# Sliding descriptor picks and a four-product tail in a two-layer convolution kernel

## The reference

```python
def spatial_descriptor(x, k):                      # k = 5
    xp = jnp.pad(x, ((0, 0), (0, 0), (2, 2), (2, 2)))
    corrs = [jnp.sum(x * dynamic_slice(xp, (0, 0, di, dj), (b, c, h, w)), axis=1)
             for di in range(k) for dj in range(k)]
    return jnp.stack(corrs, axis=1)                # 25 values at each pixel
def _L0_conv_ref(x, W, bias):
    gs = spatial_descriptor(x, 5)
    gs = gs / jnp.sqrt(jnp.sum(gs * gs, axis=1, keepdims=True) + 1e-6)
    feat = jnp.concatenate([x, gs], axis=1)        # 512 + 25 channels
    return relu(einsum('bchw,oc->bohw', feat, W) + bias)
x = x + _L0_conv_ref(_gn(x), L0_conv_W, L0_conv_bias)
x = x + _L1_conv_ref(_gn(x), ...)                  # pooling windows chosen per plane, mixed
```

## Time and profile before

| what | value |
|---|---|
| median of three runs | 4177.26 us (4173.68 to 4180.9) |
| the profiled execution, its own time | 4180.08 us |
| its span in the profile | 4177.9 us |
| busy, share of the span: TensorE | 83% |
| VectorE | 81% |
| GpSimd | 50% |
| ScalarE | 47% |
| TensorE weight loads (beside its products) | 47% |
| mean rate of all transfers | 187 GB/s |

### The profile page before, as it was taken

The page is one execution under the profiler, slowest core; times in us unless marked ns, Lnnn a source line. Parts: engine busy times, 40 slices in busy tenths (PEclk is TensorE's granted clock), DMA queues, the critical chain, the costliest instruction groups (busy, mean ns, idle before and its releaser), DMA issues. The chain is left out here.

```text
span 4177.9 us, 72982 instructions
## 1 busy us (share of the span) xinstructions
PE 3474.2 (83%) x22600; PEld 1981.8 (47%) x22601; DVE 3378.0 (81%) x3619; ACT 1981.8 (47%) x3227; POOL 2087.4 (50%) x1576
## 2 busy tenths in 40 slices
PE   4999999999999999999999996567678666666554
PEld 3666666666665666666666664223233222222221
DVE  5777777777777777777777766899989999999995
ACT  3545445445445545545445440664556544444342
POOL 3555555556555555555555541554444444454343
PEclk9999999999999999999999996878889888877777
DMA  5445445445454454455455233664478666565552
GB/s 195 154 156 185 164 157 187 158 164 181 161 175 168 165 176 166 162 177 178 147 177 187 98 128 74 258 244 186 184 293 339 269 254 244 232 247 197 222 199 81
DMA packets 252355, 782.10 MB, mean 187 GB/s; under 512 B 98150, under 2 KB 98150, under 8 KB 229990
## 3 DMA queue, kind: packets, MB, share of 16 engines
q1 hardware_dynamic: 219600, 417.85, 29.0%
q0 software_dynamic: 32288, 358.95, 21.9%
HBM read 428.22 MB, written 409.08 MB: 200 GB/s over the span
## 5 line engine op out<-in xcount | busy, mean ns | idle before, releaser
L1039 DVE TENSOR_TENSOR arena<-arena 128x2048 f32<-128x2048 f32 (+9 forms) x635 | 1454.8, 2319 | 66.4 <-issue 23.1
L439 POOL TENSOR_TENSOR arena<-arena 128x512 f16<-128x512 f32 x512 | 651.2, 1277 | 861.5 <-ACT arena L582 860.3
L1390 PE MATMUL psum<-arena 128*128 128x512 f32 x896 | 534.9, 682 | 461.5 <-issue 336.6
L448 POOL TENSOR_TENSOR arena<-arena 128x512 f32 (+1 forms) x512 | 639.7, 1271 | 293.6 <-ACT arena L594 288.2
L1219 PE MATMUL psum<-arena 128*128 128x512 f16 x2048 | 776.3, 379 | 1.0 <-ACT arena L594 1.0
L1221 PE MATMUL psum<-arena 128*128 128x512 f16 x2048 | 776.2, 379 | 0.0
L1220 PE MATMUL psum<-arena 128*128 128x512 f16 x2048 | 776.2, 379 | 0.0
L1196 PE MATMUL psum<-arena 128*128 128x256 f16 (+1 forms) x6344 | 712.7, 270 | 34.5 <-DVE arena L789 21.2
L580 ACT ACTIVATE arena<-arena,gbias,grstd 128x512 f32 (+1 forms) x512 | 413.7, 808 | 632.0 <-PE psum L1221 515.6
L1392 PE MATMUL psum<-arena 128*128 128x512 f32 x1072 | 604.5, 661 | 71.1 <-ACT psum L665 54.4
L679 ACT ACTIVATE arena<-psum 128x512 f32<-128x512 f32 x536 | 315.9, 598 | 716.4 <-PE psum L1392 704.4
(11 more groups left out here) (150 smaller groups left out, 3246.6 us busy)
## 6 DMA issues: line engine op xcount, KB each, us to landing
arena<-in_x SPq DMA_DIRECT2D x64, 2048.0 KB, 13.0
wide_planes<-arena SPq DMA_DIRECT2D x128, 1024.0 KB, 8.9
y_planes<-arena SPq DMA_DIRECT2D x64, 2048.0 KB, 7.7
arena<-arena SPq DMA_DIRECT2D x1536, 8.0 KB, 1.8
arena<-wide_planes,arena POOLq DMA_INDIRECT x72, 11.7
arena<-plane_records,arena POOLq DMA_INDIRECT x67, 7.8
arena<-y_planes,arena POOLq DMA_INDIRECT x67, 9.7
out<-arena POOLq DMA_INDIRECT x67, 9.2
```

The costliest lines, as they stand in the source:

```text
L439: pool.tensor_tensor(gl[:, ct, slot], g32[:, ct % 2, :], gh[:, ct, slot], ALU.subtract).then_inc(s_gl, 1)
L448: pool.tensor_tensor(y, y, relu[:, o % 2, :], ALU.add).then_inc(s_added, 1)
L1039: ins = dve.tensor_tensor(dst, a, b, ALU.max)
L1390: pe.matmul(dst, diag[:, s, 0, :], small[:, s, b * ROWS:(b + 1) * ROWS, 1:W + 1], start=False, stop=False, skip_group_check=True)
```

## The change

It does three things. First, `pick` becomes one table of `PICK_W` = 68 columns for each role and `e`, instead of four tables of 32; a product takes the slice of 32 that starts at `(2 * t + q) * KS`, so that each parity gets its own rows, and the rows of PSUM are the same 25 for both. Second, a product of `picks` therefore covers one parity: 48 products of 32 columns (24 at the image's edges) instead of 24 of 64, and bank `BANK_A` holds the two parities as neighbours, so that one product writes every second word. Third, `tail` needs one set of weights for both parities: four products of 512 columns instead of eight of 256, each of which writes pairs of neighbouring words, 8 words from pair to pair. The constants shrink from 1536 to 1176 columns, and `wd` and its staging from 1024 to 512.

```diff
--- before.py
+++ after.py
@@ -43,6 +43,7 @@
 REP = 3 * 32
 QUADS = 4
 QW = CW // QUADS
+PICK_W = 7 * KS + 33
 
 
 def const_arrays():
@@ -53,15 +54,14 @@
     band = (np.abs(p[:, None] % W - p[None, :] % W) <= KS // 2).astype(np.float32)
 
 
-    pick = np.zeros((P, 3, 2, QUADS, 32), np.float32)
+    pick = np.zeros((P, 3, 2, PICK_W), np.float32)
+    x = np.arange(PICK_W)
     for role in range(3):
         r, k = (p // 8 % 2, p // 16) if role == AFTER else (p // W, p % 8)
         for e in range(2):
-            for t in range(QUADS):
-                di = r + 2 * (1 - role) - e
-                rho = (k - 2 * t + 2) % 8
-                ok = (np.abs(di) <= KS // 2) & (rho < 6)
-                pick[p[ok], role, e, t, (rho * KS + di + 2)[ok]] = 1.0
+            di = r + 2 * (1 - role) - e
+            hit = x[None, :] % (8 * KS) == ((k[:, None] + 2) * KS + di[:, None] + 2) % (8 * KS)
+            pick[:, role, e, :] = hit & (np.abs(di) <= KS // 2)[:, None]
     ssum = (p[:, None] // 32 == p[None, :] // 32).astype(np.float32) * 2.0 ** -12
     gavg = (p[:, None] // CG == p[None, :] // CG).astype(np.float32) / CG
     ident = np.eye(P, dtype=np.float32)
@@ -70,7 +70,7 @@
     return np.concatenate([band, pick.reshape(P, -1), ssum, gavg, ident, before, ones], axis=1)
 
 
-CONST_W = P + 3 * 2 * QUADS * 32 + P + 4 * P
+CONST_W = P + 3 * 2 * PICK_W + P + 4 * P
 
 
 def turned_rows():
@@ -78,11 +78,9 @@
 
 
     rows = np.full((D * KS,), C, np.int64)
-    for par in range(2):
-        for rho in range(6):
-            for di in range(KS):
-                if 0 <= rho - par < KS:
-                    rows[(rho * KS + di) * 2 + par] = C + di * KS + rho - par
+    for dj in range(KS):
+        for di in range(KS):
+            rows[dj * KS + di] = C + di * KS + dj
     return rows.reshape(D, KS)
 
 
@@ -98,7 +96,7 @@
     nc.disable_value_cache = True
 
     x_v = x.rearrange("b (t p) h w -> b p t (h w)", p=P)
-    wturn_v = wturn.rearrange("a (b n) -> (a b) n", n=C)[0:64, :].rearrange("(m q) n -> m (q n)", q=2)
+    wturn_v = wturn.rearrange("a (b n) -> (a b) n", n=C)[0:32, :]
     out_rows = out.rearrange("b c h w -> (b c) (h w)")
     y_dram = nc.dram_tensor("y_planes", [NPL, PIX], fp32, kind="Internal").ap()
     y_v = y_dram.rearrange("(b t p) n -> b p t n", t=CT, p=P)
@@ -119,8 +117,8 @@
         cst = sb("cst", [P, CONST_W], fp32)
         o = 0
         band = cst[:, o:o + P]; o += P
-        pick = cst[:, o:o + 6 * QUADS * 32].rearrange("p (r e t m) -> p r e t m", r=3, e=2, t=QUADS)
-        o += 6 * QUADS * 32
+        pick = cst[:, o:o + 6 * PICK_W].rearrange("p (r e x) -> p r e x", r=3, e=2)
+        o += 6 * PICK_W
         ssum = cst[:, o:o + P]; o += P
         gavg = cst[:, o:o + P]; o += P
         ident = cst[:, o:o + P]; o += P
@@ -171,10 +169,10 @@
         wide = wide_f.rearrange("p (t h w) -> p t h w", t=CT, h=ROWS)
         wh = take(CT * C // 2).bitcast(fp16).rearrange("p (t n) -> p t n", t=CT)
         wl = take(CT * C // 2).bitcast(fp16).rearrange("p (t n) -> p t n", t=CT)
-        wd = take(2 * C // 2).bitcast(fp16)
+        wd = take(C // 2).bitcast(fp16)
 
         stage_w = arena[:, CT * PIX:CT * PIX + CT * C].rearrange("p (t n) -> p t n", t=CT)
-        stage_d = arena[:, CT * PIX + CT * C:CT * PIX + (CT + 2) * C]
+        stage_d = arena[:, CT * PIX + CT * C:CT * PIX + (CT + 1) * C]
 
 
         def xs_quarter(par, q):
@@ -1235,11 +1233,14 @@
                         half = c % 2 * PAIRS * P if role == BEFORE else 0
                         src = bq[role][:, half:half + PAIRS * P]\
                             .rearrange("p (u t q r j) -> p t r q u j", t=QUADS, q=2, r=2, j=8)
-                        for t in range(QUADS):
-                            dst = psum[32 * t:32 * t + 32, BANK_A, 0:QW]\
-                                .rearrange("p (q u r j) -> p r q u j", q=2, r=2, j=8)
-                            last = pe.matmul(dst[:, e, :, u0:u1, :], pick[:, role, e, t, :], src[:, t, e, :, u0:u1, :],
-                                             start=(e == 0 and k == 0), stop=True, skip_group_check=True)
+                        for q in range(2):
+                            for t in range(QUADS):
+                                dst = psum[32 * t:32 * t + 32, BANK_A, 0:QW]\
+                                    .rearrange("p (u r j q) -> p r q u j", q=2, r=2, j=8)
+                                at = (2 * t + q) * KS
+                                last = pe.matmul(dst[:, e, q, u0:u1, :], pick[:, role, e, at:at + 32],
+                                                 src[:, t, e, q, u0:u1, :], start=(e == 0 and k == 0 and q == 0),
+                                                 stop=True, skip_group_check=True)
                 last.then_inc(s_pick, 1)
 
             def turn_blocks(i, c):
@@ -1267,12 +1268,11 @@
 
                 half = c % 2
                 pe.wait_ge(grouped[half], (i * (CH // 2) + c // 2 + 1) * GROUPED)
-                src = tpair[0:REP, half, :].rearrange("p (t q s) -> p q t s", t=QUADS, q=2)
+                src = tpair[0:REP, half, :].rearrange("p (t s q) -> p t s q", t=QUADS, q=2)
                 for o in range(CT):
-                    dst = psum[:, o, :].rearrange("p (s t q) -> p q t s", t=QUADS, q=2)
-                    for par in range(2):
-                        last = pe.matmul(dst[:, par], wd[0:REP, par * C + o * P:par * C + (o + 1) * P],
-                                         src[:, par], start=False, stop=True, skip_group_check=True)
+                    dst = psum[:, o, :].rearrange("p (s t q) -> p t s q", t=QUADS, q=2)
+                    last = pe.matmul(dst, wd[0:REP, o * P:(o + 1) * P], src, start=False, stop=True,
+                                     skip_group_check=True)
                     last.then_inc(s_conv, 1)
 
             def group_average(i):
```

## The result

The changed kernel takes 4150.07 us (median of four runs, 4146.73 to 4152.5) against 4179.08 us for the kernel before (four runs, 4173.68 to 4183.56): a ratio of 0.993, 95% interval 0.9918 to 0.9942. It is faster by 29 us, where 64 were forecast. The profiled execution's own time is 4152.5 us, its span 4150.3.

What follows compares the result with a forecast made beforehand. TensorE was taken to set the pace in layer 0. Gain 101 us, less 33, 1 and 5 given back, plus 2 at the start: 64 us less, 4113 us; own range 4090 to 4135, chance 0.60.

Steps and rivals of the forecast that it cites:

- The tail, 0.82 us per chunk: In each chunk's tail, pairs write at full rate like `conv`: 0.86 us instead of 1.68, saving 0.82 us.
- rivals 3 and 4: Tail stays at 1.68 us: 3, picks' fp32 records pay double, 4265 us, chance 0.07; 4, picks nearly free, 4179 us, 0.08.
- The picks, 0.03 us more: In the picks block of each chunk, doubling the products adds only their non-column cost: 0.03 us, block 0.84 us.
- the lower bound by columns: Picks block: price goes by columns, 1536 as before and again 0.64 us, plus 0.03 us for 24 record groups instead of 12.
- The upper bound, 0.67: Picks block: each group of four records still costs 0.056 us with half the columns; 12 more groups, 0.67 us more.
- the 86 chunks that were to give nothing back: Chunks with room before TensorE waits for VectorE's mask, expected to keep their net saving of 0.79 us each.
- These three give all of the 0.79 back: Chunks 4, 6 and 0, where `gram` already waits for VectorE's mask, lose their saving in 14 images: 33 us.
- the wait at line 1286 [...] stays: TensorE's wait in chunk 4, 21.6 us in all, follows `norm` with no tail between, so it stays unchanged.
- In chunk 0 a second thing adds: VectorE's wait for the row-maxima store comes later against TensorE in some images: 5 us lost, from 0 to 11.
- The start, 2 us: Before the chunks, halved instructions on `wd` save some 1.3 us and shorter constants at most 1.1: 2 us taken.
- rival 2: The picks block doubles, 0.67 us more, leaving 0.15 us per chunk in 86 chunks: 4162 us; chance 0.20.

Runs made afterwards that it cites:

- experiment 4: Changed kernel, picks writing runs of eight and tail reading with a step: 4246.46 us; separately, changed kernel with BEFORE and AFTER picks cut to 16 columns: 4145.32 us.
- Experiment 1: Changed kernel, but SyncE issues the store of chunk 5's row maxima in chunk 6 ahead of the 2 MB load of x: 4106.46 us, ratio 0.9833.
- e3_best: Changed kernel with row-maxima store first, `x_stats` behind mask 3 in chunks 0, 3 and 6, `group_spreads` ahead of `wide_rows` in chunk 4: 4062.2 us, ratio 0.9715.
- the picks only: Changed kernel with new picks but eight tail products of 256 columns writing single words, as before; output not the reference's: 4206.2 us, ratio 1.0067.
- e2_before_wide_first: Kernel before the change, with the store of the row maxima issued ahead of the load of x: 4165.71 us, ratio 0.996.
- tail only: Kernel before with the new tail of four 512-column products and the old picks; output not the reference's: 4128.9 us, ratio 0.9885.

## Why the prediction was right or wrong

- **The tail, 0.82 us per chunk: right.** It takes 0.86 us, as forecast. Pairs are written at full rate; rivals 3 and 4 are out. That the two periods per column of the old tail come from its single words is argued and not shown by itself: the old tail also reads its input in runs of 64, the new one in one run of 512, and experiment 4 shows that a read pattern can cost more than either tail.
- **The Trainium skill's remark on non-contiguous patterns** ("PSUM — Partial Sum Buffer", "Specifications (TRN2)") doesn't hold for pairs in fp16 products, which take 0.216 us per 512 columns like a contiguous output, nor for every second word in fp32 products: experiment 4 shows the same block of 1.01 to 1.02 us with runs of eight and with every second word. For the tail that wrote single words, 0.210 us per 256 columns, the trace agrees with it; the 8-byte line stated there fits both.
- **The picks, 0.03 us more: mis-sized.** 0.21 measured. The step that failed is the lower bound by columns: 24 groups at 29 ns. It held down to 48 columns, but at 32 the groups stand 31 to 34 ns apart whatever the columns, and the first `gram` starts 186 ns behind the last record where it was 152. That is 86 x 0.18 = 15 us of the forecast, in the 86 chunks that were to give nothing back. The upper bound, 0.67, was far off. The Trainium skill's overhead of about 60 cycles per product ("TensorEngine Tiling (Array Packing)", "Instruction Overhead") is nearer to the mechanism than my columns were: 16 and 32 columns cost the same here. Its 60 can't mean columns in these strips, since a group takes 31 to 34 ns with 32 columns and 56 with 64.
- **"These three give all of the 0.79 back": right for chunk 6 and for the mask of chunk 4, wrong for the rest of chunk 4.** In the nine images with an ordinary chunk 5 before it, chunk 6 stays at 18.48 to 18.55 us, where it was 18.46 to 18.50; it is shorter where chunk 5 was long (images 1, 6, 8 and 13) and in image 14. In chunk 4 `gram` now waits for the mask, but "the wait at line 1286 [...] stays" was wrong. It fell from 1.53 us in the kernel before to 1.18 in the changed one, 21.6 to 17.1 us in all:

```profile
1242.99 0.38 PE L1286 MATMUL psum<-gd,cst 128*128 128x4 f32 x2 [1.53 <-DVE gd L762]
```

```profile
1216.20 2.03 PE L1194 MATMUL psum<-arena 128*128 128x256 f16 x17 [0.67 <-DVE arena L787]
...
1231.11 0.39 PE L1286 MATMUL psum<-gd,cst 128*128 128x4 f32 x2 [1.18 <-DVE gd L760]
```

  The two chunks fell by 0.35 and 0.27 us in the mean, together 14 x 0.62 = 9 us.
- **"In chunk 0 a second thing adds [...] I take 5 us in all, from 0 to 11": this is the step that failed most.** I had the store that hangs on the chunk two before, but the period of chunk 0 rose by 2.24 us, 31 us in 14 images, where I had it rise by 0.36. The waits were of the size that I bounded: VectorE's wait for the store rose by 11.5 us in these images (0.96 to 2.47 us in the two shown), where I took 5 and had 11 as the most. What I put at nothing is what a longer wait does to TensorE's own clock: 12 of these chunks have a stretch at 1.2 GHz where three had one, which is worth about 20 us (an estimate from the 44 us more at half clock, and what the waits leave of the loss); in the image shown the grams last 2.5 us longer. Experiment 1 takes the store's lateness away, and with it both.
- **Chunk 5: not foreseen.** Its mean is 0.59 us above its usual 18.25, 8 us in all. In the image with its longest chunk 5, TensorE's third and fourth `gram` waited 2.39 us for nothing that the profile shows, and then ran at half clock:

```profile
1079.99 4.45 PE L1194 MATMUL psum<-arena 128*128 128x256 f16 x24 [2.39 <-issue]
```

  Such waits stand in chunk 5 of images 1, 6, 8 and 13 (0.25, 2.39, 1.07 and 2.12 us) and of no other. TensorE's program has seven images unrolled, so 1 and 8, and 6 and 13, are the same stretch of it. That the instructions themselves come late there fits, but wasn't tested, and `e3_best`, which has the same program on TensorE, has no long chunk 5 (a mean of 18.26). The doubled picks don't explain it: with the picks only the mean of chunk 5 is 19.67 against 19.12 as a rule, but in images 1 to 14 without any such wait. Five of those chunks hold a stretch at half clock, behind the wait at the group statistics just before them. `e2_before_wide_first`, which has the old picks, shows the same in two images (20.57 against 18.90). Its `gram` in one of them, with no wait before it and a granted clock of 0.50 over most of it:

```profile
619.61 4.46 PE L1200 MATMUL psum<-arena 128*128 128x256 f16 x24
```

- **The start, 2 us: 0.6 measured** (first `picks` at 62.59 and 61.97 us).

Together: 64 - 15 (picks) - 26 (chunk 0, 1.88 x 14) - 8 (chunk 5) + 9 (chunks 4 and 6) + 3 (`norm`, 86 x 0.04) - 1 (start) = 26 us. Measured are 22.4 us from the first to the last `picks` and 0.6 at the start, 23 us; the 3 us between lie in single chunks, such as chunk 0 of image 0, which is 0.33 us longer and not shorter. The span fell by 27.6; the other 4.6 us lie behind the last `picks`, where the change hardly reaches, and weren't looked into. So the tail was forecast by its mechanism, and two steps failed: the clock behind the waits of chunk 0, put at nothing, and the price of the picks. The time fell between the forecast's own range, 4090 to 4135, and rival 2's 4162, whose picks block of 1.5 us didn't come. The losses were taken from the waits as they stood, and not from what a longer wait sets off.

## What to carry to other kernels

Before an engine that is nearly always busy is made faster, look where it waits already, however little: there the gain is given back, and the stall can grow past it, through a transfer tied to an earlier step and through TensorE's clock. A reordering of two transfers that is worth 16 us before may be worth 44 after. And count small products as products, not as columns.

## What the runs showed of the hardware

- fp16 products that write pairs of words, 8 words from pair to pair, take one clock period per column at 2.4 GHz (0.216 us for 512), like a contiguous output. The tail that wrote single words 8 apart, and read its input in runs of 64, took two (0.210 us for 256).
- fp32 products in four column strips, each with its own weights, take the time of their columns down to 48 (0.75 against 0.81 us for a block), but 31 to 34 ns per four records at 32 and at 16 columns alike, against 56 ns at 64.
- Reading the moving operand with a step of 64 fp16 elements between neighbours, with the output in the same pairs, took 0.48 us per 512 columns instead of 0.216: more than any write pattern here.
- The end of VectorE's loop took 1.8 us between chunks 7 and 0 and 4.8 us between 2 and 3, in the mean.
- A wait of 3.60 us was followed by a granted clock of 0.50, and so was one of 1.98 us; waits of 3.70 and of 1.28 us weren't (the 24 grams behind each took 2.79 us, as at 2.4 GHz). The chunks 0 of images 1 to 14 had 3 stretches at 0.50 with 22.0 us of waits in all (before), 12 with 42.6 (changed), 6 with 41.1 (tail only) and none with 17.4 (experiment 1).
